# Spreading the expert gates with a selection matmul instead of a DMA broadcast

## The reference

```
logits = ht @ router_w                                  # layer 3; layer 2 is alike, with its own weights
probs  = softmax(logits); topv, topi = top_k(probs, K)  # K = 6 of 16 experts (layer 2), 2 of 8 (layer 3)
w_dense[token, topi] = topv                             # (layer 3: divided by their sum)
g = einsum('td,edf->tef', ht, w_gate)
u = einsum('td,edf->tef', ht, w_up)
eo = einsum('tef,efd->ted', silu(g) * u, w_down)
moe = einsum('te,ted->td', w_dense, eo)                 # layer 3 adds a shared expert without a gate
```

## Time and profile before

| | |
|---|---|
| median of 3 runs | 2347.95 us (2340.27 to 2348.03) |
| the profiled execution: its own time | 2347.95 us |
| the profiled execution: span of the core | 2345.6 us |
| mean granted TensorE clock | 0.958 of full speed |
| PE, DVE, ACT, POOL busy | 94%, 66%, 45%, 59% of the span |
| layer 2's expert stage begins | 1568.1 us |
| layer 3's expert stage begins | 2265.3 us |

### The profile page before, as it was taken

How to read it: one execution, slowest core, us unless ns; L and a number is a source line. 1 busy time by engine, 2 the same in 40 slices (tenths; PEclk the granted TensorE clock), 3 DMA queues, 4 the chain that set the end, 5 groups by cost and what they waited for, 6 DMA issues and landing times.

```text
span 2345.6 us, 31158 instructions
## 1 busy us (share of the span) xinstructions
PE 2209.3 (94%) x11484; PEld 1551.9 (66%) x11484; DVE 1542.6 (66%) x2502; ACT 1064.5 (45%) x1573; POOL 1391.7 (59%) x901
## 2 busy tenths in 40 slices
PE   7789999899999997798999999989998999999988
PEld 5578888765665655565556656567886666656587
DVE  6766652478878856765878877652334788788653
ACT  4453443554555544311455555443434545555443
POOL 0352210278888874366688888824443888888744
PEclk9898999999999998799899999998999999999989
DMA  3124655211111103100121121015531111111022
GB/s 90 48 62 138 196 161 160 82 40 40 54 47 40 41 16 125 42 1 11 50 60 40 40 59 41 7 46 148 151 105 54 40 40 58 42 40 46 6 63 75
DMA packets 55394, 152.76 MB, mean 65 GB/s; under 512 B 8453, under 2 KB 14421, under 8 KB 54860
## 3 DMA queue, kind: packets, MB, share of 16 engines
q1 hardware_dynamic: 54860, 150.44, 21.3%
q10 hardware_dynamic: 384, 0.33, 0.1%
HBM read 135.88 MB, written 14.86 MB: 64 GB/s over the span
## 4 chain that ended last, share of the span: by engine, by line
PE 82%; DVE 7%; POOL 3%; ACT 2%; DMA 2%; issue 2%; SPq 0%; POOLq 0%; ACTq 0%; DVEq 0%
PE psum L890 20%; PE psum L1365 19%; PE psum L1355 10%; PE psum L1336 10%; PE psum L1357 10%; PE psum L1521 2%; PE psum L1476 2%; PE psum L1382 2%; POOL CL L1808 1%; PE psum L1250 1%; PE psum L1544 1%; PE psum L1128 1%; DMA WqrT<-in_a_WrT 1%; DMA bd<-in_blockdiag 1%; DVE mx L2333 1%
## 5 line engine op out<-in xcount | busy, mean ns | idle before, releaser
L1786 ACT ACTIVATE E<-psum 125x896 f32<-125x896 f32 x576 | 528.3, 920 | 581.1 <-PE psum L1357 554.2
L2336 DVE TENSOR_REDUCE mx<-psum 128x1 f32<-128x500 f32 x945 | 611.8, 675 | 171.9 <-PE psum L1336 170.0
L2085 POOL TENSOR_TENSOR SA<-SA,E 125x896 f32<-125x896 f32 x282 | 597.1, 2117 | 22.1
L1365 PE MATMUL psum<-E,V 125*64 125x448 f32 x2304 | 472.2, 545 | 0.0
L1355 PE MATMUL psum<-Q,K 128*125 128x448 f32 x1152 | 331.5, 369 | 2.3 <-ACT E L1786 2.3
L1336 PE MATMUL psum<-K,Q 128*128 128x500 f32 x945 | 328.7, 402 | 3.1 <-DVE Q L2274 1.9
L1357 PE MATMUL psum<-Q,K 128*125 128x448 f32 x1152 | 329.8, 367 | 0.0
L1365 PEld LDWEIGHTS psum<-E,V 125*64 125x64 f32 x2304 | 152.9, 136 | 228.6 <-issue 223.3
L2085 POOL TENSOR_TENSOR SA<-SA,SB 125x896 f32<-125x896 f32 x93 | 194.3, 2089 | 153.6 <-DVE SB L2359 153.6
L1336 PEld LDWEIGHTS psum<-K,Q 128*128 128x128 f32 x945 | 174.2, 188 | 134.1 <-issue 33.1
L1355 PEld LDWEIGHTS psum<-Q,K 128*125 128x125 f32 x1152 | 213.2, 187 | 37.1 <-ACT E L1786 6.9
(11 more groups left out here) (303 smaller groups left out, 3712.8 us busy)
## 6 DMA issues: line engine op xcount, KB each, us to landing
K<-kt_scratch SPq DMA_DIRECT2D x48, 750.0 KB, 4.9
K<-kt_scratch SPq DMA_DIRECT2D x48, 375.0 KB, 6.0
EW<-in_f_w SPq DMA_DIRECT2D x64, 256.0 KB, 6.3
kt_scratch<-kt SPq DMA_DIRECT2D x16, 750.0 KB, 4.3
WS<-in_f_w SPq DMA_DIRECT2D x31, 384.0 KB, 4.8
GB<-gates_scratch SPq DMA_DIRECT2D x36, 224.0 KB, 3.7
WoT<-in_a_WoT SPq DMA_DIRECT2D x24, 256.0 KB, 3.1
V<-in_ctx SPq DMA_DIRECT2D x16, 375.0 KB
```

The lines of the kernel that those rows point to most:

```text
L1365: i = e.matmul(psum[c * DC:(c + 1) * DC, 4 + b % 2, 0:HT], V[0:LP, b, k * DC:(k + 1) * DC], E[g[n, b, k] % NE][0:LP, half[c]], start=k == ...
L1786: e.activation(E[m % NE][0:LP, :].rearrange("p (c q) -> p c q", c=2), psum[0:LP, pair:pair + 2, 0:HT], ACT.Exp).then_inc(exp_set.sem, 1)
L2085: e.tensor_tensor(SA[b % 2][0:LP, :], a[0:LP, :], x[0:LP, :], ALU.add).then_inc(sum_set.sem, 1)
L2336: e.tensor_reduce(mx[:, b % 2, j * 3 + c:j * 3 + c + 1], psum[:, bank, 0:CW], AX.X, ALU.max).then_inc(small_free.sem, 1)
```

## The change

The gate rows no longer go through DRAM. A constant 0/1 table `sel2` (64 x 2816, 704 KB) or `sel3` (64 x 8, 2 KB) is loaded at the start of the stage and copied by ACT into `selr`, in the rounded format that PE takes in one pass, at the place of `route 1`. GT becomes a tile of that format with the rounded gates in rows 0 to n-1 and the remainder of the rounding in rows 32 to 31+n. For each gated block and half, a new PE task `sel` multiplies 48 (layer 2) or 40 (layer 3) rows of `selr` with GT: one matmul of 448 columns, whose 128 output rows are the gates of the block. DVE multiplies HF by that PSUM bank. All `gload` tasks, the scratch tensor and the GB tiles go; `sel` takes a place in the ring of banks, which DVE's gate product (`gated`) frees. There are 44 such matmuls in layer 2 and 16 in layer 3. Gates 0 and 1 both stand in slot 3, where before they stood in slots 3 and 4.

```diff
+    rows = np.arange(64)[:, None] % 32
+    c["sel2"] = (rows == np.arange(E2 * I2)[None, :] // I2).astype(f)
+    c["sel3"] = (rows == np.arange(E3)[None, :]).astype(f)
...
-            if k == 2:
-                order += [("gload", n) for n in range(free, free + 3)]
-        for x in {2: (), 3: (0,), 4: (1, 2)}.get(k, (k - 2,)):
+        for x in {2: (), 3: (0, 1)}.get(k, (k - 2,)):
             if 0 <= x < len(slots):
-                n, c = slots[x]
-                order.append(("gate", n, c))
-                order += [("gload", n + 3)] if c == 1 and free <= n < blocks - 3 else []
+                order.append(("gate", *slots[x]))
...
+        elif t[0] == "gate":
+            out += [("sel", *t[1:])] if t[1] >= FFN_FREE[f] else []
...
     def sp_experts(e, f):
         m = ffn[f]
+        if f != 0:
+            e.dma_start(m["sel"][:, :], io[f"sel{f}"]).then_inc(sel_in.sem(f), 16)
...
-            elif kind == "gload":
-                n, = t
-                x = n - FFN_FREE[f]
-                if x == 0:
-                    e.wait_ge(*gt_set.at(f, 1))
-                    e.dma_start(GS[f - 2, 0:(E2 if f == 2 else E3), :], m["GT"][0:(E2 if f == 2 else E3), :]).then_inc(gs_out.sem(f), 16)
-                    e.wait_ge(*gs_out.at(f))
-                if x >= 3:
-                    e.wait_ge(*gated.at(f, n - 3, 1))
-                for rows, one_gate in gate_rows(f, x):
-                    e.dma_start(m["GB"][x % 3][rows, :],
-                                GS[f - 2, one_gate:one_gate + 1, :].broadcast_to([rows.stop - rows.start, T])).then_inc(gb_in.sem(f, n), 16)
...
+            elif kind == "gate" and t[0] >= free:
+                n, c = t
+                bank = upper(e, f, "sel", n, c)
+                if (n, c) == (free, 0):
+                    e.wait_ge(*gt_set.at(f, 1))
+                    e.wait_ge(*sel_set.at(f))
...
+                e.matmul(psum[:, bank, 0:HT], pick_e, m["GT"][0:rows, half[c]], start=True, stop=True).then_inc(gates_made.sem, 1)
...
+            elif kind == "route" and f != 0 and t[0] == 1:
+                e.wait_ge(*sel_in.at(f))
+                e.activation(m["selr"][:, :], m["sel"][:, :], ACT.Copy).then_inc(sel_set.sem, 1)
...
-                e.memset(ffn[n]["probs"][:, :, :], BIG).then_inc(*dve_own.up())
+                e.memset(ffn[n]["probs"][:, :, :], BIG)
+                e.memset(ffn[n]["GT"][:, :].bitcast(F32), 0.0).then_inc(*dve_own.up())
...
-            e.tensor_copy(m["GT"][0:n, cols], psum[0:n, bank, 0:w]).then_inc(gt_set.sem, 1)
+            e.tensor_copy(m["GT"][0:n, cols], psum[0:n, bank, 0:w]).then_inc(*dve_own.up())
+            e.wait_ge(*dve_own.now())
+            e.tensor_tensor(m["GT"][32:32 + n, cols], psum[0:n, bank, 0:w], m["GT"][0:n, cols].bitcast(F32),
+                            ALU.subtract).then_inc(gt_set.sem, 1)
...
-                if c == 0:
-                    e.wait_ge(*gb_in.at(f, n))
-                e.tensor_tensor(hf, hf, m["GB"][(n - free) % 3][:, half[c]], ALU.mult).then_inc(gated.sem, 1)
+                e.wait_ge(*gates_made.at(f, n, c))
+                e.tensor_tensor(hf, hf, psum[:, upper_bank[f, ("sel", n, c)], 0:HT], ALU.mult).then_inc(gated.sem, 1)
```

More of the change, by code:

```diff
@@ L168, in expert_order @@
     slots = [(n, c) for n in range(blocks) for c in range(2)]
-    order, free = [("fetch", n) for n in range(4)] + [("split", 0), ("split", 1), ("route", 0)], FFN_FREE[2 if blocks == NB2 else 3]
+    order = [("fetch", n) for n in range(4)] + [("split", 0), ("split", 1), ("route", 0)]
     side = list(side)
@@ L192, in expert_order @@
         if k < len(slots):
-            n, c = slots[k]
             if side and k >= 2:
@@ L664, in build @@
         at(base)
-        m["GB"] = [mem.take("GB", [P, T], F32) for _ in range(3)]
+        wide = E2 * I2 if f == 2 else E3
+        m["selr"] = mem.take("selr", [64, wide], F32R)
         m["HF"] = [mem.take("HF", [P, HT], F32) for _ in range(4)]
+        high_at = mem.at
         m["HH"], m["HL"] = ([mem.take(n, [P, HT], F32R) for _ in range(4)] for n in ("HH", "HL"))
+        high_end = mem.at
+        at(high_at if f == 2 else high_end)
+        m["sel"] = mem.take("sel", [64, wide], F32)
+        assert f == 3 or mem.at <= high_end
+        at(max(high_end, mem.at))
         m["lmax"], m["lexp"] = mem.take("lmax", [P, NT], F32), mem.take("lexp", [P, NT, n_exp], F32)
@@ L671, in build @@
         m["w"], m["wsum"] = mem.take("w", [P, NT, n_exp], F32), mem.take("wsum", [P, NT], F32)
-        m["GT"] = mem.take("GT", [P, T], F32)
+        m["GT"] = mem.take("GT", [P, T], F32R)
         if f == 2:
@@ L675, in build @@
         assert mem.at <= w1_at
-    GS = nc.dram_tensor("gates_scratch", (2, E2, T), F32, kind="Internal").ap()
     def done(order, *kinds):
@@ L765, in build @@
     lt_made, lt_set = (flag(n, done(FFN[0], "logits")) for n in ("logits_t_made", "logits_t_set"))
-    w_set = flag("w_set", [(f,) for f in (2, 3)])
+    sel_set, w_set = (flag(n, [(f,) for f in (2, 3)]) for n in ("sel_set", "w_set"))
     gt_halves = [(f, a) for f in experts for a in range(2)]
@@ L773, in build @@
     prod_set = flag("prod_set", [u for u in ups if SWIGLU[u[0]]])
+    gates_made = flag("gates_made", [u for u in per_ffn("gate") if u[1] >= FFN_FREE[u[0]]])
     gated = flag("gated", [u for u in per_ffn("gate") if u[1] >= FFN_FREE[u[0]]])
@@ L845, in build @@
     heads_in = Landed(nc, "heads", 4, [(g, (g,)) for g in range(4)], 2)
-    gate_in, gs_out = one("gate_w", 1, [(f,) for f in experts]), one("gates_out", 1, [(f,) for f in (2, 3)])
-    gb_in = Landed(nc, "", 3, [((n - FFN_FREE[f]) % 3, (f, n)) for f, n in per_ffn("gload")], 2, after=wq_in)
+    gate_in, sel_in = one("gate_w", 1, [(f,) for f in experts]), one("sel", 1, [(f,) for f in (2, 3)])
     slots_in = one("slots")
@@ L859, in upper_free @@
             return prod_set.at(f, n, c) if k else r_set.at(f, n, c)
-        if kind == "turn_gates" or kind == "back":
-            return {"turn_gates": gt_set, "back": x_back}[kind].at(f, *key)
+        if kind == "turn_gates" or kind == "sel" or kind == "back":
+            return {"turn_gates": gt_set, "sel": gated, "back": x_back}[kind].at(f, *key)
         if kind == "ynorm":
@@ L1436, in pe_experts @@
     def pe_experts(e, f):
-        m, blocks, swiglu = ffn[f], FFN_BLOCKS[f], SWIGLU[f]
+        m, blocks, free, swiglu = ffn[f], FFN_BLOCKS[f], FFN_FREE[f], SWIGLU[f]
         n_exp = {0: E0, 2: E2, 3: E3}[f]
@@ L1444, in pe_experts @@
                     pe_up(e, f, *t)
+            elif kind == "gate" and t[0] >= free:
[4 more added lines that the diff above has]
+                    e.wait_ge(*sel_set.at(f))
+                x = n - free
+                if f == 2:
+                    rows = 32 + E2
+                    pick_e = m["selr"][0:rows, x * P:(x + 1) * P]
+                else:
+                    rows = 32 + E3
+                    pick_e = m["selr"][0:rows, x:x + 1].broadcast_to([rows, P])
+                e.matmul(psum[:, bank, 0:HT], pick_e, m["GT"][0:rows, half[c]], start=True, stop=True).then_inc(gates_made.sem, 1)
             elif kind == "down":
```

## The result

The changed kernel takes 2363.51 us (median of 5 runs, 2361.47 to 2369.79) against 2347.95 before. The ratio, taken over all runs of both kernels and not only over these, is 1.0079 with a 95% interval of 1.0063 to 1.0094. That is slower by 0.8%, and the median is above the range forecast (2340 to 2361). The profiled execution took 2367.42 us with a span of 2365.6, 20.0 us longer than the span before; the granted clock, as a mean over the span, is 0.960 against 0.958, so the clock explains nothing of it.

The account below looks back on a forecast made before the run. PE was taken as the bound, 82% of the chain, with a 10.2 us wait for WqrT. On 2347.95 us, 57 further `sel` add 11.4 and the earlier start takes 7.9: 2351.5 us, range 2340 to 2361.

Parts of the forecast that it names:

- What the change adds on PE: Both expert stages: 60 `sel` matmuls at the stream's 0.20 us each, 12.0 us in all.
- The bound above: Upper cost of one `sel` on PE: a matmul's own duration, 0.36 to 0.37 us, if it overlapped with no neighbour.
- The sum: Whole kernel: 57 further `sel` add 11.4 us, less 7.9 at layer 2's start: +3.5, 2351.5 us.
- The start: Layer 2's expert stage: WqrT wait goes, late table stalls PE up to 4 us, slot 5 starts 7.9 us earlier.
- DVE, ACT, POOL and the ring: Steady slots: gate product waits for nothing, tighter ring of PSUM banks costs nothing, with about 2 us cover per slot.
- Small edits: GT's memset, layer 3's small table and its subtractions hide in existing waits; uncovered, the subtractions cost up to 1.3 us.
- Rival 2: A `sel` breaks PE's stream and costs its whole 0.37 us: +13.2, 2361 us; chance 10%.
- Rival 1: Layer 2's start: table to 64 partitions lands some 4 us later, shifting everything up to slot 4: 2355.5 us; chance 15%.
- Rivals 3 and 4: 3: slack in steady slots makes `sel` cost little, 2340 us, 10%; 4: clock kept through the new stall, 2349.6 us, 15%.

Follow-up runs that it names:

- e1: The changed kernel with every `sel` padded with zeros from 48 or 40 to 128 rows of weights; 2345.65 us, ratio 1.0008 to the kernel before.
- e3: The changed kernel with every `sel` matmul issued twice in a row to the same bank; 2382.99 us in one run.
- e2: The changed kernel with 64 rows of weights in each `sel` in place of 48 or 40; 2365.03 us in one run.
- e5: As e1, but each `sel` takes 65 rows instead of 128; 2345.33 us in one run.
- e6: e1 with layer 2's table fetched and copied in two pieces, the first 256 columns ahead; 2334.8 us, ratio 0.9981 to the kernel before.
- e4: The kernel before with only the attention folding's first group of loads moved to slot 0, gates still by DMA; 2335.94 us, ratio 0.9976.
- e7: e4 with `sel` of full 128-row tiles for layer 2's block 0 alone, other gates by DMA; 2328.76 us, ratio 0.995 to the kernel before.
- e8: The same kernel as e4, run again in the second batch beside e7; 2334.75 us, ratio 0.9979 to the kernel before.

## Why the prediction was wrong

Its steps one by one.

- **What the change adds on PE, 0.20 us per `sel`: this is the step that failed.** "I take the value of the stream, since a `sel` is issued like any other matmul" doesn't hold for a tile of 48 rows between tiles of 128. A `sel` costs 0.58 us, of which 0.20 are the matmul (e1, e3) and 0.38 the two changes of shape (e1, e2, e5). The bound above, 0.36 to 0.37, was too low as well: it took the worst case to be a matmul that overlaps with no neighbour, but a stop is not bounded by a matmul's duration. The step named the hole itself ("no row shows a matmul with 48 rows of weights") and then didn't look for the nearest rows in that respect, the fold's 64-row and 64-column groups.
- The rule that it weighed, of the Trainium skill ("TensorE: Matmul & The Clock Gate", LDWEIGHTS), that a load's time goes by its columns, holds for the load: 183 ns with 48 rows, 187 with 128. It says nothing of the gap ahead of the load. The rule that speaks against the change stands on another page ("TensorEngine Tiling (Array Packing)", Key Properties) and was not weighed; the runs agree with it: 0.19 us per change with 40, 48 and 64 rows, none with 65.
- **The sum.** 57 `sel` at 0.57 to 0.58 are 32.5 us (23.2 for 41, the wait for HL that went taken off; 9.3 for 16) in place of 11.4: +21.1. The rest takes back 4.6: the start +0.4 (7.44 earlier, not 7.87), the stretch between the stages -1.9, layer 3's stage -3.3 (below), +0.2 ahead. Forecast +3.5, so 20.0 us come out, which is what the spans show. The stretch between the stages has the same code before and after; it took 485.0 to 490.4 us in the ten traces, so the -1.9 is no effect of the change.
- **The start: right, each step within 1.6 us.** The table landed 6.0 us after its issue, not 4.6; copy 2.55 (2.57 said), R ends 1578.7 (1577.2), PE's wait for R 3.69 (up to 4), `up` of slot 3 at 1579.91 (1578.6), slot 5 at 1590.04 (1589.45). Half clock lasted only to about 1582.4, which gave 1.3 us back in this `up` and in the folding group behind it: slot 4 started at 1584.99 (1585.0). e6 confirms that the table is what made the stall.
- **DVE, ACT, POOL and the ring: right.** From 1592 to the last `down` of layer 2 PE waits for none of them, though each slot got tighter.
- **Small edits: right where they were hidden, with one miss.** "The DMA wait of layer 3's first gate product was never PE's" stands. What the prediction missed is a wait of 0.93 us for HL in the tail of each stage (1768.92 and 2330.25 before), though it says that from 1597.32 on no wait of any length is left. It is there in all traces with gates by DMA (before, e4, e7, e8) and in none where all gated blocks have a `sel`, and no gate product waits for a load there: HL comes late by way of DVE, ACT and POOL behind the last `up`, and in e1 the `sel` of the last three gate products stand in the gap (2323.39, 2324.82, 2326.24). So the change's matmuls are partly free there. Layer 3's first `down` came 13.3 us after its stage's start and not 13.5, though a `sel` (0.6) was added ahead of it, since PE waited 0.64 us for the gate transposes' input and not 1.23. The last 1.6 us are no effect of the change: the final output landed 4.1 us after its issue and not 5.7, and in e3, which has the same loads as the changed kernel, its issue is again 6.3 us from the end, against 4.5.
- **Rival 2 was right in what happens** and had 10%: "A `sel` breaks the stream", decided from 0.34 us each. The price it set, 0.37, was a matmul's duration, and too low by 0.2 us. Against it the prediction set "that weight loads hide everywhere in these slots"; they don't, as the fold's rows of before show.
- Rival 1 (the table late by 4 us) was off: 1.4 us late. Rivals 3 and 4: no slack in the steady slots (e1 adds 0.20 us per `sel`), and the clock was not kept (0.50 granted behind the stall).

What the change was worth apart from this: the order of the loads alone gains about 5 us (e4, e8), e1's 128 rows make the change neutral (1.0008), e6 takes it to 0.9981, and leaving the gates of all blocks but the first to the idle DMA queues (e7) to 0.995.

## What to carry to other kernels

Before a matmul goes into a dense stream, compare its stationary tile's shape with its neighbours': with 48 or 64 rows between tiles of 128 it cost 0.38 us beyond its own 0.20, and padding the contraction with zeros, to 128 rows or only to 65, cost nothing on PE. Two such matmuls side by side pay the 0.38 us once. Where a prediction says "no row shows this shape", search the trace for the nearest rows in that very respect (here, few rows or columns of weights) and read the idle time ahead of them and the spacing of the starts, not their duration alone. And when a wait is put down to a load, first try the order of the loads by itself: here it gained more than the change did, and showed which single block needed the new way.

## What the runs showed of the hardware

That 48 and 64 rows stop the stream and 65 do not, with the load's own time unchanged, was not in the prediction (e2, e5). A second thing: one DVE product of 112 columns took 1.79 us or 0.28 us. The timelines of the kernel before (POOL, DVE) and then of e6 (DVE, POOL):
```profile
1573.26 1.96 POOL L2123 TENSOR_TENSOR WL<-WS,WH 128x768 fp32r<-128x768 f32 x1 [11.17 <-ACT WH L1864]
1573.56 1.79 DVE L2563 TENSOR_TENSOR w<-probs,expert_mask 128x112 f32<-128x112 f32 x1
```
```profile
1570.37 0.28 DVE L2586 TENSOR_TENSOR w<-probs,expert_mask 128x112 f32<-128x112 f32 x1
1570.38 1.96 POOL L2139 TENSOR_TENSOR WL<-WS,WH 128x768 fp32r<-128x768 f32 x1 [2.94 <-ACT WH L1871]
```
In the kernel before, e4, e7 and e8 it starts 0.3 us into POOL's subtraction of 1.96 us and ends about when that ends; in e6 it starts just ahead of it, in e1 and the changed kernel while POOL is idle, and takes 0.28. A gate product shows the same in e8, where it reads HF and GB, both in SBUF. POOL subtracts from 1582.12 to 1583.94. The timeline of DVE:
```profile
1582.94 2.01 DVE L2598 TENSOR_TENSOR HF<-HF,GB 128x448 f32<-128x448 f32 x2
```
Of these two products the first takes 1.48 us, where 0.62 is usual. A product with one input in PSUM is not slowed: in the changed kernel the one that starts at 1579.89, inside POOL's subtraction (1579.57 to 1581.40), takes its 0.62 us. So a DVE operation on two SBUF inputs appears to be held while POOL works on such inputs. This is read from seven traces and was not tested by a run of its own. It matters little here: PE waits 0.7 us for the small product before, and not at all for it in e6.
